# Attention steps with the out-projection between query tiles, scores by heads, and earlier splits in the last MLP batch

## The reference

```
xn   = layernorm(x)                                  # over the last axis
q,k,v = xn wq^T, xn wk^T, xn wv^T                    # 16 query heads, 4 key/value heads, 128 wide
q,k  = rope(q), rope(k)
o_h  = causal linear attention of head h, weight exp(-lam_h * (i - j)) for j <= i   # no softmax
s    = o wo^T
g    = silu(down(silu(gate(xn)) * up(xn)))           # MLP 512 -> 1536 -> 512, weights rounded to fp8 values
out  = x + s * g
```

## Time and profile before

| | |
|---|---|
| median of 3 runs | 993.4 us (991.66 to 994.18) |
| the profiled execution, its own time | 990.39 us |
| its span, first to last instruction | 988.6 us |
| mean granted clock of PE in it | 0.983 |

### The profile page before, as it was taken

How to read it: one execution, slowest core, us unless ns; L and a number is a source line. 1 busy time by engine, 2 the same in 40 slices (tenths; PEclk the granted TensorE clock), 3 DMA queues, 4 the chain that set the end, 5 groups by cost and what they waited for, 6 DMA issues and landing times.

```text
span 988.6 us, 12631 instructions
## 1 busy us (share of the span) xinstructions
PE 919.1 (93%) x4192; PEld 758.2 (77%) x4192; DVE 628.4 (64%) x875; ACT 426.8 (43%) x725; POOL 415.1 (42%) x299
## 2 busy tenths in 40 slices
PE   4899999999986899999999999999999999898986
PEld 3688888888865778787787877878778787686866
DVE  7877632112233384867968668778684786869686
ACT  3445333223242454454554544646345364443521
POOL 2011132222244554645546555464554655535451
PEclk9999999999998899999999999999999999999999
DMA  5833030410110340202312112223020240443324
GB/s 184 309 113 111 11 129 1 170 43 1 68 61 0 128 149 1 85 23 106 129 56 94 43 43 85 82 89 121 27 85 0 85 156 13 162 116 111 102 54 139
DMA packets 20057, 86.10 MB, mean 87 GB/s; under 512 B 2480, under 2 KB 3632, under 8 KB 16560
## 3 DMA queue, kind: packets, MB, share of 16 engines
q1 hardware_dynamic: 20016, 85.56, 25.0%
HBM read 68.78 MB, written 16.78 MB: 87 GB/s over the span
## 4 chain that ended last, share of the span: by engine, by line
PE 36%; issue 30%; POOL 20%; DVE 10%; ACT 2%; DMA 1%; SPq 0%; POOLq 0%; DVEq 0%; ACTq 0%
PE bank L1009 35%; POOL d_r L962 12%; POOL rot L971 8%; DVE d_sb L785 1%; DVE rot L760 1%; DVE q_r L766 1%; DVE rot L759 1%; DVE acc L845 1%; DMA rot<-mlp_gate 1%; ACT q_r L462 1%; PE bank L1019 1%; DVE d_sb L831 0%; DMA stage<-in_x_nat 0%; DVE d_sb L776 0%; DVE acc L843 0%
## 5 line engine op out<-in xcount | busy, mean ns | idle before, releaser
L1009 PE MATMUL bank<-xn,aw 128*128 128x512 f32 x1152 | 273.2, 393 | 0.5 <-DVE aw L667 0.5
L962 POOL TENSOR_TENSOR d_r<-d_sb,d_r 128x512 fp32r<-128x512 f32 x160 | 218.8, 1381 | 117.8 <-ACT d_r L507 115.8
L1009 PEld LDWEIGHTS bank<-xn,aw 128*128 128x128 f32 x1152 | 215.8, 189 | 46.5 <-issue 1.4
L971 POOL TENSOR_TENSOR rot<-rot 128x512 f32<-128x512 f32 x80 | 129.4, 1617 | 210.1 <-DVE rot L760 210.1
L1009 PE MATMUL bank<-xn,gu_w 128*128 128x512 f32 x768 | 183.0, 394 | 4.0 <-DVE fz L662 1.7
L1009 PE MATMUL bank<-o_r,ow 128*128 128x512 f32 (+1 forms) x816 | 182.6, 377 | 0.0
L1009 PEld LDWEIGHTS bank<-xn,gu_w 128*128 128x128 f32 x768 | 145.6, 190 | 35.9 <-DVE dn_w L654 2.1
L507 ACT CAST d_r<-d_sb 128x512 fp32r<-128x512 f32 x160 | 97.1, 619 | 166.1 <-DVE d_sb L831 136.1
L1009 PEld LDWEIGHTS bank<-o_r,ow 128*128 128x128 f32 x816 | 145.9, 188 | 27.3
L759 DVE TENSOR_TENSOR rot<-bank,rope 128x512 f32<-128x512 f32 x80 | 54.8, 684 | 95.7 <-ACT rot L475 95.5
L1009 PE MATMUL bank<-fsplit,dn_w 128*128 128x512 f32 x384 | 100.5, 408 | 11.7 <-POOL fsplit L943 11.7
(11 more groups left out here) (69 smaller groups left out, 857.2 us busy)
## 6 DMA issues: line engine op xcount, KB each, us to landing
xn<-xn_split SPq DMA_DIRECT2D x15, 2048.0 KB, 7.8
xn_split<-xn SPq DMA_DIRECT2D x4, 2048.0 KB, 8.9
wst<-in_mlp_w SPq DMA_DIRECT2D x10, 768.0 KB, 4.5
stage<-in_attn_w SPq DMA_DIRECT2D x4, 1536.0 KB, 6.5
stage<-in_x_nat SPq DMA_DIRECT2D x16, 256.0 KB, 4.7
mlp_gate<-gout SPq DMA_DIRECT2D x16, 256.0 KB, 2.9
stage<-in_out_w SPq DMA_DIRECT2D x4, 1024.0 KB, 4.8
stage<-in_x_t SPq DMA_DIRECT2D x15, 256.0 KB, 5.2
```

What stands on the lines that cost most here:

```text
L962: pool.tensor_tensor(d_r[:, e % SRING, 1, :], d_sb[:, e % SRING, :], d_r[:, e % SRING, 0, :].bitcast(F32), ALU.subtract).then_inc(d_lo, 1)
L971: pool.tensor_tensor(rot1[:, r % RRING, :], rot1[:, r % RRING, :], rot2[:, r % RRING, :], ALU.add).then_inc(qk_sum, 1)
L1009: last = pe.matmul(dst, a, b, start=start and x == 0, stop=stop and x == len(pairs) - 1)
```

## The change

Six edits, in the diff below with its repetitions cut:

1. ACT and POOL issue the splits of the last MLP batch earlier than the turns, sums and casts of the attention's tiles. PE's order there stays.
2. PE's out-projection pieces 0, 1 and 2 stand behind projection tiles 3, 4 and 5 of the next step, and piece 3 ahead of the scores; before, 0 and 1 stood behind tile 5, 2 behind `state` and 3 behind `inter`.
3. DVE's `accumulate` (and `finish`) of piece u stands behind the rotation of tile u + 3, and the last behind the score blocks.
4. `out_ps[2]` is bank 1, which tile 3 used, in place of bank 4.
5. The two score blocks of two heads each come first, and each waits for its own heads.
6. The waits of projection tiles 0 and 1 and of out-projection 2 follow the banks.

```diff
-BLOCKS = [(3, 0, HG, 3, 1), (2, 0, 2, 2, 2), (2, 2, 2, 2, 2), (0, 0, HG, 1, 1), (1, 0, HG, 1, 1), (0, 0, HG, 0, 1)]
+BLOCKS = [(2, 0, 2, 2, 2), (2, 2, 2, 2, 2), (3, 0, HG, 3, 1), (0, 0, HG, 1, 1), (1, 0, HG, 1, 1), (0, 0, HG, 0, 1)]
...
-        out_ps = [bank[5], bank[0], bank[4], bank[5]]
+        out_ps = [bank[5], bank[0], bank[1], bank[5]]
...                                       # ACT, last MLP batch
-            projections(0, {1: [lambda: fuse_hi(first + 3)], "k": [lambda: fuse_hi(first + 4)],
-                            3: [lambda: fuse_hi(first + 5), lambda: fuse_hi(first + 6)],
-                            4: [lambda: fuse_hi(first + 7), lambda: fuse_hi(first + 8)],
-                            QK: [lambda: fuse_hi(first + 9), lambda: fuse_hi(first + 10), lambda: fuse_hi(first + 11)],
+            projections(0, {1: [lambda: fuse_hi(first + 3), lambda: fuse_hi(first + 4)],
+                            "k": [lambda: fuse_hi(first + 5)], 2: [lambda: fuse_hi(first + 6)],
+                            3: [lambda: fuse_hi(first + 7), lambda: fuse_hi(first + 8)],
+                            4: [lambda: fuse_hi(first + 9), lambda: fuse_hi(first + 10)],
+                            QK: [lambda: fuse_hi(first + 11)],
...                                       # DVE, step
+                def collect(u):
+                    accumulate(n, g, b, u)
+                    if final and u < KT - 1:
+                        finish(n, b, u)
...
+                    after = {r: [lambda u=r - 2: collect(u)] for r in (2, 3, 4)}
+                    projections(n + 1, g + 1 if edge else g, g + 1 if edge else None, beside, after)
...
-                for u in range(KT):
-                    if u == 2:
-                        st_rest(n + 1)
-                    if u == KT - 1:
-                        for t in range(HEAD):
-                            decay_block(n + 1, t)
-                    accumulate(n, g, b, u)
-                    if final and u < KT - 1:
-                        finish(n, b, u)
+                st_rest(n + 1)
+                for t in range(HEAD):
+                    decay_block(n + 1, t)
+                collect(KT - 1)
...                                       # PE, project and scores
-                elif tile < 2:
-                    pe.wait_ge(acc_d, (n - 1) * KT + 3 + tile)
+                elif tile == 0:
+                    pe.wait_ge(rot_d, n * QK)
+                elif tile == 1:
+                    pe.wait_ge(acc_d, (n - 1) * KT + KT)
...
-                elif t == 0:
-                    pe.wait_ge(qk_lo, n * QK + QK)
-                    if_later(n, lambda: pe.wait_ge(acc_d, n * KT + 2))
+                else:
+                    pe.wait_ge(qk_lo, n * QK + 1 + h0 + nh)
+                    if t < 2:
+                        if_later(n, lambda: pe.wait_ge(acc_d, n * KT + 2 + t))
...                                       # PE, step
-                projections(n + 1, g_edge)
-                pe.wait_ge(o_lo, n * NOT + NOT)
-                if start:
-                    pe.wait_ge(ow_lo, g * HG + HG)
-                for u in range(KT):
-                    if u == 2:
-                        state(n + 1)
-                    if u == KT - 1:
-                        for t in range(HEAD):
-                            scores(n + 1, t)
-                        inter(n + 1)
-                    out_projection(n, g, u)
+                projections(n + 1, g_edge, beside={3: [first_out], 4: [lambda: out_projection(n, g, 1)],
+                                                   5: [lambda: out_projection(n, g, 2)]})
+                state(n + 1)
+                out_projection(n, g, KT - 1)
+                for t in range(HEAD):
+                    scores(n + 1, t)
+                inter(n + 1)
```

More of the change, by code:

```diff
@@ L31 @@
           (slice(0, HG), slice(P, 2 * P)), (slice(0, HG), slice(0, P))]
-ODONE = [1, 2, 4, 5]
-OF_BLOCK = [None, 0, 1, 2, 2, 3]
+ODONE = [2, 2, 4, 5]
+OF_BLOCK = [0, 1, None, 2, 2, 3]
 NOT = len(OTILES)
@@ L796, in st_rest, with projections @@
                                   st_r[:, 0, :, :].bitcast(F32), ALU.subtract).then_inc(st_lo, 1)
-            def projections(n, g, tables=None, beside={}):
+            def projections(n, g, tables=None, beside={}, after={}):
                 for other in beside.get(0, ()):
@@ L817, in projections @@
                         q_decay_head(n, r - 2)
+                    for other in after.get(r, ()):
+                        other()
                 qk_rest(n, QK - 1)
@@ L902, in step @@
                         beside = {r: [lambda h=h: ow_split_lo(g, h) for h in hs] for r, hs in ((0, (0, 1, 2)), (1, (3,)))}
-                    projections(n + 1, g + 1 if edge else g, g + 1 if edge else None, beside)
+                    after = {r: [lambda u=r - 2: collect(u)] for r in (2, 3, 4)}
+                    projections(n + 1, g + 1 if edge else g, g + 1 if edge else None, beside, after)
                 if last:
@@ L993, in _ @@
             fuse_rest(first + 1)
[L994 to L998, removed]
+            projections(0, {1: [lambda: fuse_rest(first + 2), lambda: fuse_rest(first + 3), lambda: fuse_rest(first + 4)],
+                            2: [lambda: fuse_rest(first + 5), lambda: fuse_rest(first + 6)],
+                            "v": [lambda: fuse_rest(first + 7), lambda: fuse_rest(first + 8)],
+                            4: [lambda: fuse_rest(first + 9), lambda: fuse_rest(first + 10)],
+                            VD + QK: [lambda: fuse_rest(first + 11)]})
             for t in range(HEAD):
@@ L1161, in inter, with projections @@
                     last.then_inc(d_used, 1)
-            def projections(n, g_edge=None, skip_first=1):
+            def projections(n, g_edge=None, skip_first=1, beside={}):
                 for tile in range(skip_first, PT):
@@ L1168, in projections @@
                         transpose_k(n)
+                    for other in beside.get(tile, ()):
+                        other()
             def scores(n, t):
@@ L1188, in times_v @@
                 pe.wait_ge(d_lo, n * NEL + e + 1)
-                if t == 0:
+                if OF_BLOCK[t] is None:
                     for x in range(2):
                         tile = o_ps[x][:].rearrange("p (h c) -> p h c", h=2)[:, :, P:HALF]
-                        last = products(tile, pairs(slice(x * HALF, (x + 1) * HALF)), start=False, stop=False)
+                        last = products(tile, pairs(slice(x * HALF, (x + 1) * HALF)), start=False, stop=True)
                     last.then_inc(d_used, 1)
@@ L1215, in out_projection @@
                 elif u == 2:
-                    pe.wait_ge(rot_d, n * QK + 2 * QK)
+                    pe.wait_ge(rot_d, n * QK + QK + 3)
                 else:
@@ L1234, in step, with first_out @@
                     return
-                projections(n + 1, g_edge)
-                pe.wait_ge(o_lo, n * NOT + NOT)
-                if start:
-                    pe.wait_ge(ow_lo, g * HG + HG)
-                for u in range(KT):
-                    if u == 2:
-                        state(n + 1)
-                    if u == KT - 1:
-                        for t in range(HEAD):
-                            scores(n + 1, t)
-                        inter(n + 1)
-                    out_projection(n, g, u)
+                def first_out():
+                    pe.wait_ge(o_lo, n * NOT + NOT)
+                    if start:
+                        pe.wait_ge(ow_lo, g * HG + HG)
+                    out_projection(n, g, 0)
+                projections(n + 1, g_edge, beside={3: [first_out], 4: [lambda: out_projection(n, g, 1)],
[5 more added lines that the diff above has]
+                inter(n + 1)
             first = (NB - 1) * MT
```

## The result

The changed kernel takes 959.23 us (median of 4 runs, 958.96 to 960.42), the kernel before 993.79 beside it. The ratio is 0.9656, with a 95% interval of 0.9635 to 0.9676. Forecast were 961, a range of 950 to 974, and faster at 0.94. The span of the profiled execution is 957.2 us, where the sum said 956.8.

What follows compares the result with a forecast made beforehand. PE was taken as the bound, busy 39.25 of 40.70 us in a steady step. Span 988.6 - 17.8 - 12 - 2 = 956.8, 958.6 as profiled time, plus 3.0 for the runs' median: 961 us, range 950 to 974.

Steps and rivals of the forecast that it cites:

- Splits of the last batch: End of the MLP stage: earlier splits remove three PE waits of 3.9 us and slow clock; gain 17.8 us.
- The steady step: Twelve steps of groups 0 to 2: 40.70 to 39.7 us each, a 0.45 us wait left; gain 12 us.
- The final steps: Three final steps: old 3.94 us wait gives way to 3.1 + 0.8 + 0.5; gain 2 us for the three.
- the store's wait: Final steps: piece 2's add waits for piece 0's store, landing at 33.5; nothing, or 1 us, in two of three.
- A collision of DVE and POOL in the steady step: First rival: the two engines collide in steady steps, whose gain is 0; time 973, chance 0.15.
- the second rival: Final steps keep pace if DVE's early pieces fall where POOL is idle: 946 us, chance 0.14.
- the third rival: Final steps get worse, `finish` waiting for POOL or the store later than 33.5: 970 us, chance 0.12.
- The total: Whole profiled span: 988.6 less 17.8, 12 and 2 gives 956.8 us.

Runs made afterwards that it cites:

- this half alone: Kernel before plus only the earlier ACT and POOL splits of the last MLP batch, steps as before: 975.98 us, ratio 0.9837.
- finish late: Changed kernel with the two finish operations of out-projection piece 2 behind the three decay blocks in the final steps: 950.11 us, second set 949.96.
- the second of the halves: Changed kernel with edit 1 undone, so only the new order of the steps: 975.35 us, ratio 0.9831.
- last-piece kernel: Changed kernel with out-projection piece 3 put back behind `inter`: 997.26 us, ratio 1.0054 to the kernel before.
- Scores by heads: Changed kernel, but each of the first three score blocks waits for all heads: 959.86 us.
- store-first kernel: Changed kernel with SP's store of piece 0 ahead of `load_xn` in the final steps: 952.4 us, ratio 0.9588 to the kernel before.
- `late = (1, 2)`: Changed kernel with finish operations of pieces 1 and 2 both behind the three decay blocks in the final steps, store in its old place: 955.83 us.
- `late = (1, 2)` and the store first: Changed kernel with finish of pieces 1 and 2 behind the decay blocks and SP's store of piece 0 ahead of `load_xn`: 952.99 us.

## Why the prediction was right, point by point

*Splits of the last batch.* Right in mechanism and size: 17.5 us in the trace for 17.8, the 0.33 us for slab 11 included, and 16.3 in the kernel with this half alone. What I had not seen is the clock behind it. Before, `state(0)` followed a wait of 2.56 us and ran its six matmuls in 1.62 us, at full clock. After, it follows a wait of 2.86 us and runs at the lower of the two levels (1.2 GHz), in 2.90 us. The changed kernel's busy time over that stretch, with the granted clock third from the end:

```profile
315.29:318.00 2.71, 2.71 (x7) 2.13 (x8) 0.00 (x0) 0.00 (x0) 0.00 (x0) 0.50 1.19 304
```

That takes back 1.3 us. It is no property of the change: the kernel with finish late has the same instructions there and a wait of 2.89, and ran the six in 1.63 (below). The kernel without the new splits, the second of the halves, took 2.77 for them behind the old wait of 2.56.

```profile
314.50 1.63 PE L1018 MATMUL bank<-d_r,kn_r 128*128 128x512 f32 x6 [2.89 <-issue]
```

*The steady step.* The mechanism held event by event: the last head 5.4 us later, its rest ready at 31.0 and asked for at 32.0, `inter` just covered, and one new wait at the first `times_v`. In the trace the key tile starts at 365.32; the other engines' rows of that step, in the changed kernel's timeline, are

```profile
395.18 1.18 DVE L767 TENSOR_TENSOR q_r<-rot,q_r 128x512 fp32r<-128x512 f32 x1
...
396.64 2.20 PE L1013 MATMUL bank<-q_r,k_r 128*128 128x512 f32 x9
...
397.94 0.69 DVE L796 TENSOR_TENSOR st_r<-bank,st_r 128x512 fp32r<-128x512 f32 x1 [1.25 <-ACT st_r L496]
...
398.86 1.69 PE L1013 MATMUL bank<-d_r,st_r 128*128 128x256 f32 x12
...
399.97 6.31 POOL L966 TENSOR_TENSOR d_r<-d_sb,d_r 128x512 fp32r<-128x512 f32 x5 [1.17 <-ACT d_r L507]
```

The head's rest ends at 396.36, 31.0 after the key tile, and the second block is asked for 0.68 behind 396.64. `st_rest` ends at 398.63 and `inter` starts at 398.86. The term was mis-sized: 15.1 us for 12, or 1.26 a step for 1.0. The wait at `times_v` is about 0.2 us where I put 0.45, since POOL's first rest is there 0.14 us earlier than I added up (35.9 for 36.05) and PE asks 0.15 later, and the twelve old steps average 40.84 us, not the 40.70 of the one I had read. The last-piece kernel shows what this rests on: piece 3 as cover for the last head is worth 2.4 us a step.

*Scores by heads.* Costed at nothing, without a sentence of its own; measured at nothing.

*The final steps.* The forecast named the right wait, the second score block on the last head's rest, and its size roughly: 3.1 forecast, 4.33 and 4.38 in the two steps with a `load_xn`, 1.98 in the third. Behind it I had put 0.8 us for `st_r` at `inter`; in the first two steps no such wait is there, since the six matmuls ahead of it ran at the low clock and PE asked later; in the third it is 0.71.

Two numbers of the forecast were off, in opposite directions. DVE's own work costs about 2 us of wait and not 3.1: that is what both the third step and the store-first kernel show. And the store's wait was put at "nothing, or 1 us" and was 2.65. The step that failed there is first the landing: I had 7.8 us for `load_xn` and 1 more for the store; issued 0.4 us behind it, the store took 10.0 us, where it takes 2.5 in front of it, and so landed 35.1 us into the step, not at 33.5. And DVE was ready for the add at 32.5, not 33.8. These 1.6 and 1.3 us, less the 0.3 of slack that I had, make the wait of 2.65. The order of the two transfers costs 6.2 us in the final part. The ring order that the Trainium skill states ("DMA: Bandwidth & Descriptors", Queues, rings and completion order) agrees with 10.0 against 2.5; its caution that completion is not first in, first out brought the store nothing here.

The steps themselves were not 0.7 us shorter each: the first went from 45.74 to 45.09, the second from 44.80 to 46.42, so it got longer, and the third gained 2.7. Traces of the same code differ here too: the final part is 157.4 and 156.3 us in two kernels with the old steps, and 156.4 and 155.0 in two with the new, so the 1.1 us that the whole change gained in the final part is no more than that scatter.

*The rivals.* A collision of DVE and POOL in the steady step did not decide, though DVE's operations ahead of the asking took nearly the long durations that I had charged: 1.51 us for the decayed head, as put, and 1.18 for the last rest where I put 1.30. Against the second rival I had set "over 12 us of idleness at the step's start"; that is a misreading, since the earlier trace rows leave DVE only 10.4 us idle in the whole step. The late store was part of the third rival and happened, but only two steps had it, and the time stayed at the forecast since the third step gained 2.7 us (38.04 for 40.70 to the last step's scores). The exclusive lock that the Trainium skill states ("SBUF — State Buffer", Who interferes with whom), by which whoever of the two starts first keeps the shared ports for its whole instruction and the other blocks, is seen in the trace of the kernel with `late = (1, 2)`. Beside POOL's three rests the finish operations take 1.5 to 1.8 us in place of 0.69, and the rests take 4.70 us in place of 3.79. The views below are the three rests, the first of DVE's operations beside them, and the second rest by itself:

```profile
836.15 4.70 POOL L971 TENSOR_TENSOR d_r<-d_sb,d_r 128x512 fp32r<-128x512 f32 x3 [1.17 <-ACT d_r L507]
...
836.53 1.47 DVE L855 TENSOR_TENSOR stage<-acc,stage 128x512 f32<-128x512 f32 x1
```

```profile
837.41 1.74 POOL L971 TENSOR_TENSOR d_r<-d_sb,d_r 128x512 fp32r<-128x512 f32 x1
```

The first rest, with nothing ahead of it, takes 1.29 us; the DVE operation that starts during it ends about 0.55 us behind it, at 838.00, and the next two DVE operations end just as far behind the second and the third rest. Those two rests take 1.74 us each. So the engines take turns by whole instructions, which agrees with the page, and in a row of such operations both lose.

*The total.* 31.8 forecast and 31.4 measured in the span is partly luck: 3.1 us too little forecast for the gain of the steps is offset by 0.3 too much for the splits, 0.9 too much for the final part, the 1.3 of clock, and 1.0 of a later start of the attention that has nothing to do with the change.

## What to carry to other kernels

When the bound engine loses time to a wait for late work of the others, look for a piece of its own work that needs nothing new and put it directly ahead of the asking; here 2.7 us of out-projection ahead of the scores decide between 42.0 and 39.6 us a step. A piece moved forward on one engine moves what it triggers, too: list the transfers whose issue moves and what small transfer is now queued behind a large one on the same queue. And where an engine has both urgent and idle stretches, move its operations nobody waits for out of the urgent one, but look at the last iteration by itself, where the cover of the next is missing.

## What the runs showed that was not expected

The MLP stage does not take the same time in two executions of the same code, while the steady steps do. The same kernel (finish of piece 2 late) reached its first attention tile at these two times in two profiled executions:

```profile
270.66 2.88 PE L1018 MATMUL bank<-xn,aw 128*128 128x512 f32 x12
```

```profile
275.12 2.88 PE L1018 MATMUL bank<-xn,aw 128*128 128x512 f32 x12
```

The difference arises in the first 46 us. The first matmul comes 0.7 us later in the second execution, the next waits add 1.0, and one row of 48 matmuls adds 2.8; these are its views in the two:

```profile
28.52 11.50 PE L1018 MATMUL bank<-xn,gu_w 128*128 128x512 f32 x48 [1.64 <-DVE xn L627]
```

```profile
30.19 14.27 PE L1018 MATMUL bank<-xn,gu_w 128*128 128x512 f32 x48 [1.72 <-DVE xn L627]
```

The granted clock over that row was 1.00 in the first and 0.79 in the second, so most of the difference is clock and not data that came late.

From `state(0)` to the end they took 634.0 and 634.1 us, but by two differences that cancel: 9.4 and 10.7 to the next key tile, 474.9 and 474.8 for the twelve steps, 149.7 and 148.7 for the final part. So 4.5 us of the difference between two runs of one kernel can arise before the part under study, and about 1 us inside it. Cutting the spans at the same instruction shows where a difference lies, which medians of five runs do not. Whether a wait is followed by the low clock is also no function of its length alone: behind a wait of 2.86 us at the same place the six matmuls of `state(0)` took 2.90 us in the changed kernel and 1.63 in the one with `late = (1, 2)` and the store first. What else decides it was not tried.
